# A two-layer transformer kernel: attention heads regrouped over row and column quarters of TensorE, softmax of layer 0 normalised at the output, and a new written order

## What is computed

```python
# layer 0: 16 heads of 16
h = ln(x) * (scale1 + 1) + shift1
q, k, v = split(h @ Wqkv.T + bias)
qn = q / norm(q) * sm ; kn = k / norm(k)
p = softmax(qn @ kn.T + attn_bias) ; x = x + ((p @ v) @ Wproj.T + bproj) * gamma1
u = (ln(x) * (scale2 + 1) + shift2) @ Wfc1.T + bfc1
x = x + (gelu_tanh(u) @ Wfc2.T + bfc2) * gamma2
# layer 1: 8 query heads of 32, one key/value head
h = rms(x) * w * (1 + t @ tw.T)
q, k = rope(h @ Wq.T), rope(h @ Wk.T) ; v = h @ Wv.T
x = x + (softmax(q @ k.T / sqrt(32)) @ v) @ Wo.T
h = rms(x) * w2 * (1 + t @ tw2.T)
x = x + (silu(h @ Wg.T) * (h @ Wu.T)) @ Wd.T
```

## Time and profile before

| | before |
|---|---|
| median of 3 runs | 386.43 us |
| lowest and highest | 386.29, 393.18 us |
| span of the profiled execution | 387.1 us |
| mean granted TensorE clock | 0.907 |
| TensorE busy | 326.0 us, 84% |
| VectorE busy | 256.0 us, 66% |
| ScalarE busy, GpSimd busy | 199.8 us each, 52% |

### The profile page before, as it was taken

One profiled execution on the slowest core, in us unless ns is written; L12 is line 12 of the kernel. 1 busy time (PEld: TensorE's weight loads), 2 busy tenths in 40 slices (PEclk: granted clock), 3 DMA queues, 4 the chain that ended last, 5 costly groups with the idle time before them and its releaser, 6 DMA issues.

```text
span 387.1 us, 6924 instructions
## 1 busy us (share of the span) xinstructions
PE 326.0 (84%) x2240; PEld 262.6 (68%) x2240; DVE 256.0 (66%) x652; ACT 199.8 (52%) x681; POOL 199.8 (52%) x363
## 2 busy tenths in 40 slices
PE   4491575788868986998999999789999999998986
PEld 3261353466655875886776888567788888897975
DVE  3774889887889878657868785755864635434250
ACT  3234268657666688877645885643535525322110
POOL 6536958976687788258858655645522401302000
PEclk9985588576988996998999999969999999999999
DMA  7979130000000000002010000000000000000000
GB/s 219 215 242 322 56 128 10 27 2 1 1 2 1 2 3 1 2 2 54 3 55 0 2 3 1 3 0 0 2 1 3 14 15 0 15 14 2 28 2 27
DMA packets 14035, 14.27 MB, mean 37 GB/s; under 512 B 1568, under 2 KB 12960, under 8 KB 14000
## 3 DMA queue, kind: packets, MB, share of 16 engines
q1 hardware_dynamic: 14000, 13.83, 12.0%
HBM read 12.76 MB, written 1.06 MB: 36 GB/s over the span
## 4 chain that ended last, share of the span: by engine, by line
PE 61%; DVE 16%; POOL 10%; issue 6%; DMA 3%; SPq 2%; ACT 2%; DVEq 0%; POOLq 0%; ACTq 0%
PE ps_linear L1377 16%; PE ps_hidden L1200 7%; PE ps_output L1337 6%; PE ps_hidden L1202 5%; PE ps_hidden L1201 5%; PE ps_scores L1307 5%; PE ps_probs L1314 4%; PE ps_linear L1347 3%; DVE z L1115 2%; DVE qk_pack L1053 2%; DMA res_bias<-in_bfc 2%; PE ps_linear L1200 2%; PE ps_turn L1228 1%; DVE xn L978 1%; PE ps_linear L1202 1%
## 5 line engine op out<-in xcount | busy, mean ns | idle before, releaser
L733 POOL TENSOR_TENSOR z<-z,row_inv 128x512 f32<-128x512 f32 (+1 forms) x64 | 54.8, 859 | 61.8 <-DVE row_inv L1129 61.7
L836 ACT ACTIVATE z<-z,neg_max 128x128 f32<-128x128 f32 x128 | 49.6, 391 | 19.9 <-DVE neg_max L1118 19.8
L848 ACT ACTIVATE probsT<-ps_probs 128x512 f32<-128x512 f32 (+1 forms) x64 | 31.0, 485 | 35.3 <-PE ps_probs L1314 35.1
L1314 PE MATMUL ps_probs<-ident,z 128*128 128x128 f32 x192 | 36.6, 305 | 7.1 <-POOL z L733 6.3
L884 ACT ACTIVATE g_a<-ps_hidden 128x256 f32<-128x256 f32 x32 | 12.3, 384 | 45.7 <-PE ps_hidden L1202 45.5
L697 POOL TENSOR_TENSOR h_lo<-xn,h_hi 128x256 fp32r<-128x256 f32 x32 | 25.9, 812 | 18.0 <-ACT h_hi L799 17.8
L1314 PEld LDWEIGHTS ps_probs<-ident,z 128*128 128x128 f32 x192 | 25.5, 157 | 13.0 <-issue 9.6
L1377 PE MATMUL ps_linear<-Wfc2T,g_h 128*128 128x256 f32 x128 | 31.7, 404 | 1.0 <-DVE res_t L1142 0.8
L1377 PE MATMUL ps_linear<-WdT,g_h 128*128 128x256 f32 x128 | 29.4, 383 | 3.2 <-DVE g_h L1171 2.7
L839 ACT ACTIVATE z<-ps_scores,neg_max_s 128x128 f32<-128x128 f32 x64 | 23.0, 368 | 14.5 <-DVE neg_max_s L1123 14.4
L1377 PEld LDWEIGHTS ps_linear<-Wfc2T,g_h 128*128 128x128 f32 x128 | 25.1, 201 | 5.9 <-DVE res_t L1142 1.0
(11 more groups left out here) (150 smaller groups left out, 973.5 us busy)
## 6 DMA issues: line engine op xcount, KB each, us to landing
gamma<-gamma_scratch SPq DMA_DIRECT2D x8, 256.0 KB, 4.2
stage<-in_Wada SPq DMA_DIRECT2D x6, 256.0 KB, 7.2
X<-in_x SPq DMA_DIRECT2D x4, 256.0 KB, 6.9
stage<-in_Wqkv SPq DMA_DIRECT2D x4, 256.0 KB, 5.0
Wfc2T<-in_Wfc SPq DMA_DIRECT2D x1, 1024.0 KB, 11.0
stage<-in_Wfc SPq DMA_DIRECT2D x4, 256.0 KB, 6.2
WdT<-in_Wd SPq DMA_DIRECT2D x1, 1024.0 KB, 6.5
stage<-in_Wg SPq DMA_DIRECT2D x4, 256.0 KB, 2.7
```

The costliest lines, as they stand in the source:

```text
L733: pool.tensor_tensor(z[:, d, 0:U, :], z[:, d, 0:U, :], row_inv[:, d, 0:U].unsqueeze(2).to_broadcast([P, U, P]), ALU.mult).then_inc(probs_r ...
L836: ins = act.activation(z[:, d, u, :], z[:, d, u, :], ACT.Exp, bias=neg_max[:, d, u:u + 1], accum_out=total)
L848: act.activation(probsT[:, G % 2, 0:U, :], bank_of(key)[:, 0:U * P].rearrange("p (u q) -> p u q", u=U), ACT.Copy).then_inc(is_freed(key)[0 ...
L1314: ins = pe.transpose(bank[:, u * P:(u + 1) * P], z[:, G % DEEP, u, :], ident[:, :])
```

## The change

- Scores: one step U makes two groups. They lie in two row quarters and go to two banks (`ps_scores[0]`, `ps_scores[1]`), and the calls alternate between the two. The two banks are filled and freed together. 32 steps in all, 16 a layer, for 64 before.
- Groups: layer 0 has four groups of four heads an item as before, layer 1 two groups of four heads for four groups of two. The heads of a group are chosen so that the values go to four column quarters in turn.
- Softmax in layer 0: VectorE adds the mask (`mask_add`) and takes the maximum (`row_max`), now two steps; GpSimd adds the negated maximum to z (`max_off`); ScalarE takes one exponential over the whole group without sums. The probabilities are turned unnormalised. `values` multiplies them by v and, in a second part, by a block of ones, so that the row sums come to lie in the output bank beside the output; VectorE inverts them and multiplies (`attn_norm`, in the place of `attn_copy`). `row_inverse` and `norm_probs` are left in layer 1 only.
- Layer 1: the factor 1/sqrt(32) is put into Wq when the chunk is split, and the scaling of the maxima goes.
- `norm_mod` of layer 0 moves from VectorE to ScalarE. `gelu_poly` goes; `gelu_inner` does its work in one fused operation, and the constant goes into the scale of the tanh.
- Waits on the item two before become waits on the last item of the same layer. Rows of Wproj and Wo are permuted on the host, outside the timed program.
- The assumed durations, all due times (`ATT_BASE`, `MLP_BASE`, `CHUNK_SHIFT`, `SHIFT`) and the assumed time for a wake-up are new, and so is the order on every engine. Of `SHIFT`, which is not printed: qk_sum goes from -55.5 to -267.0, qk_root from -6.5 to -47.0, weight_high from 29.5 to 835.0, weight_low from -14.5 to -1.0, and max_off is -44.0.

```diff
-ATT_BASE = [-163.5, -31.5, 33.5, 66.5, 63.0, 93.0, 88.0, 127.0]
-MLP_BASE = [-0.9, 42.5, 89.5, -132.5, 129.5, 140.5, 103.5, 230.0]
-CHUNK_SHIFT = {'Wkv': -113.5, 'tw2': -105.0, 'tw1': 45.0, 'Wfc1': -217.0, 'ada': 48.0, 'Wq': 21.5, 'Wqkv':
-    40.5, 'Wg': -8.5, 'Wu': -138.0}
+ATT_BASE = [-86.0, -62.0, -34.0, 2.5, 2.5, 16.5, 160.5, 383.5]
+MLP_BASE = [-93.5, 19.5, 31.0, 48.5, 150.0, -670.5, 498.0, 828.5]
+CHUNK_SHIFT = {
+    'Wfc1': 2080.5, 'Wkv': 257.0, 'Wq': 77.0, 'Wg': -1910.0, 'Wu': 360.0, 'Wqkv': 255.0, 'ada': -45.5,
+    'tw1': -1095.5, 'tw2': 880.0}
...
-              "scores": ["scores0", "scores1"], "probs": ["probs"], "output": ["output"]}
+              "scores": ["scores"], "probs": ["probs"], "output": ["output"]}
...
-WAKE = 0.19
+WAKE = 0.26
...
-def heads_of(group):
-
-    i = group % 4
-    tiles = H0 // 4 if layer_of(group // 4) == 0 else H1 // 4
-    return [4 * g + i for g in range(tiles)]
+GROUPS = [(n, u, b) for n in range(2 * len(ROUNDS)) for u in range(2) for b in range(2 - layer_of(n))]
+
+
+def groups_of(n):
+    return [G for G, g in enumerate(GROUPS) if g[0] == n]
+
+
+def heads_of(G):
+
+    n, u, b = GROUPS[G]
+    if layer_of(n) == 0:
+        return [4 * g + 2 * u + b for g in range(4)]
+    return [4 * g + 2 * u + c for c in range(2) for g in range(2)]
 
 
...
+            for G in groups_of(n):
+                _, u, b = GROUPS[G]
+                big, U = layer == 0, 2 * n + u
+                first, last = G == groups_of(n)[0], groups_of(n)[-1]
+                g = base + 5 + GROUP_US * (4 * j + 2 * u + b)
+                if b == 0:
+                    add(("scores", U), "PE", 0.62 if big else 0.6, [ready, prev(("scores",), U)], "scores", at=g)
+                if big:
+                    add(("mask_add", G), "DVE", 0.62, [("scores", U), prev(("row_max",), G, 2), prev(("probs_turn",), G, DEEP)]
+                        + ([("mask_add", G - 1)] if b else []), frees=("scores", U) if b else None, at=g)
+                    add(("row_max", G), "DVE", 0.62, [("mask_add", G), prev(("row_max",), G)], at=g)
+                    add(("max_off", G), "Pool", 1.0, [("row_max", G)], at=g)
+                else:
+                    add(("row_max", G), "DVE", 0.68, [("scores", U), prev(("row_max",), G), prev(("probs_turn",), G, DEEP)],
+                        at=g)
+                add(("exp", G), "ACT", 0.55 if big else 1.45, [("max_off" if big else "row_max", G), prev(("exp",), G)],
+                    frees=None if big else ("scores", U), at=g)
+                if not big:
+                    add(("row_inverse", G), "DVE", 0.085, [("exp", G), prev(("row_inverse",), G)], at=g)
+                    add(("norm_probs", G), "Pool", 1.0, [("row_inverse", G), prev(("norm_probs",), G)], at=g)
+                add(("probs_turn", G), "PE", 0.535, [("exp" if big else "norm_probs", G), prev(("probs_turn",), G)],
                     "probs", at=g)
...
-                add(("values", G), "PE", 0.35 if big else 0.18, [("probs_copy", G), prev(("values",), G)]
-                    + ([("v_copy", n)] if big else []), "output" if i == 0 else None, at=g)
+                add(("values", G), "PE", 0.62 if big else 0.35, [("probs_copy", G), prev(("values",), G)]
+                    + ([("v_copy", n)] if big else []), "output" if first else None, at=g)
...
+            add(("attn_copy", n), "DVE" if layer == 0 else "ACT", 0.75 if layer == 0 else 0.27, [("values", last), prev(("attn_copy",), n), prev(("project",), n, 2)],
...
+            for e in range(2):
+                for half in range(2):
+                    pool.memset(ones_pad[:, e, half * D0:(half + 1) * D0], 1.0 if half == e else 0.0)
...
+            def max_off(G):
+                d = G % DEEP
+                pool.wait_ge(max_ready, G + 1)
+                pool.tensor_tensor(z[:, d, :, :], z[:, d, :, :], neg_max[:, d, :].unsqueeze(2).to_broadcast([P, 4, P]),
+                                   ALU.add).then_inc(max_taken, 1)
+
             def norm_probs(G):
-                U, d = len(heads_of(G)), G % DEEP
-                pool.wait_ge(inv_ready, G + 1)
-                pool.tensor_tensor(z[:, d, 0:U, :], z[:, d, 0:U, :],
-                                   row_inv[:, d, 0:U].unsqueeze(2).to_broadcast([P, U, P]),
+                d = G % DEEP
+                pool.wait_ge(inv_ready, group_ord(G) + 1)
+                pool.tensor_tensor(z[:, d, :, :], z[:, d, :, :], row_inv[:, d, :].unsqueeze(2).to_broadcast([P, 4, P]),
                                    ALU.mult).then_inc(probs_ready, 1)
 
...
+                if CHUNKS[c][0] == "Wq":
+                    act.activation(raw, raw, ACT.Copy, scale=SCORE_SCALE1).then_inc(wq_scaled, 1)
+                    act.wait_ge(wq_scaled, 1)
...
+                    dst, src = h_full[:, m, j, ft, :], bank_of(key)[:, ft * P:(ft + 1) * P]
+                    if layer_of(n) == 0:
+                        ins = act.activation(dst, src, ACT.Identity, bias=modul[:, first + 1, ft, s:s + 1],
+                                             scale=modul[:, first, ft, s:s + 1])
...
-                key = ("scores", G)
+                d = G % DEEP
+                if layer_of(GROUPS[G][0]) == 0:
+                    act.wait_ge(max_taken, group_ord(G) + 1)
+                    act.activation(z[:, d, :, :], z[:, d, :, :], ACT.Exp).then_inc(exp_ready, 1)
+                    return
                 act.wait_ge(max_ready, G + 1)
-                d = G % DEEP
-                for u in range(len(heads)):
-                    total = row_sum[:, d, u:u + 1]
-                    if layer_of(n) == 0:
-                        ins = act.activation(z[:, d, u, :], z[:, d, u, :], ACT.Exp,
-                                             bias=neg_max[:, d, u:u + 1], accum_out=total)
-                    else:
-                        ins = act.activation(z[:, d, u, :], bank_of(key)[:, u * P:(u + 1) * P], ACT.Exp,
-                                             bias=neg_max_s[:, d, u:u + 1], scale=SCORE_SCALE1, accum_out=total)
+                for u in range(4):
+                    ins = act.activation(z[:, d, u, :], ps_scores[u // 2][:, (u % 2) * P:(u % 2 + 1) * P], ACT.Exp,
+                                         bias=neg_max[:, d, u:u + 1], accum_out=row_sum[:, d, u:u + 1])
                 ins.then_inc(exp_done(G)[0], 1)
...
-                    act.activation(g_a[:, o % 2, :], g_a[:, o % 2, :], ACT.Tanh, scale=GELU_C).then_inc(g_tanh, 1)
+                    act.activation(g_a[:, o % 2, :], g_a[:, o % 2, :], ACT.Tanh, scale=GELU_CUBE).then_inc(g_tanh, 1)
...
+            def mask_add(G):
+                b, key = GROUPS[G][2], scores_key(G)
                 if G >= DEEP:
...
+                if b == 0:
+                    dve.wait_ge(*is_filled(key))
+                ins = dve.tensor_tensor(z[:, G % DEEP, :, :], ps_scores[b][:, :].rearrange("p (u k) -> p u k", u=4),
+                                        bias_mask[:, :].unsqueeze(1).to_broadcast([P, 4, P]), ALU.add)
+                ins.then_inc(mask_added, 1)
+                if b == 1:
+                    dve.wait_ge(mask_added, group_ord(G) + 1)
+                    dve.sem_inc(is_freed(key)[0], 1)
+
+            def row_max(G):
+                d = G % DEEP
+                if layer_of(GROUPS[G][0]) == 0:
+                    dve.wait_ge(mask_added, group_ord(G) + 1)
+                    dve.tensor_reduce(neg_max[:, d, :], z[:, d, :, :], AX_X, ALU.max, negate=True).then_inc(max_ready, 1)
+                    return
+                if G >= DEEP:
+                    dve.wait_ge(*is_filled(("probs_turn", G - DEEP)))
+                dve.wait_ge(*is_filled(scores_key(G)))
+                for b in range(2):
+                    ins = dve.tensor_reduce(neg_max[:, d, 2 * b:2 * b + 2],
+                                            ps_scores[b][:, 0:2 * P].rearrange("p (u k) -> p u k", u=2), AX_X, ALU.max,
+                                            negate=True)
+                ins.then_inc(max_ready, 1)
...
+            def attn_norm(n):
+                key, o = ("values", groups_of(n)[0]), ord0(n)
+                dve.wait_ge(*values_done(n))
+                dve.reciprocal(o_inv[:, :], bank_of(key)[:, C:2 * C]).then_inc(sum_inverted, 1)
+                dve.wait_ge(sum_inverted, o + 1)
+                if n >= 2:
+                    dve.wait_ge(*is_filled(("project", n - 2)))
+                dve.tensor_tensor(o_full[:, n % 2, :, :].rearrange("p c q -> p (c q)"), bank_of(key)[:, 0:C],
+                                  o_inv[:, :], ALU.mult).then_inc(is_freed(key)[0], 1)
...
-                dve.wait_ge(g_poly, o + 1)
-                dve.tensor_tensor(g_a[:, o % 2, :], g_b[:, o % 2, :], g_u[:, o % 2, :], ALU.mult
-                                  ).then_inc(g_inner, 1)
+                dve.wait_ge(g_squared, o + 1)
+                dve.scalar_tensor_tensor(out=g_a[:, o % 2, :], in0=g_a[:, o % 2, :], scalar=1.0 / 0.044715,
```

(56 more changed lines are left out.)

256 lines of the change are left out of this document (112 added, 144 removed), and 3 rows, old and new, of the table SHIFT.

## The result

The changed kernel took 361.84 us (median of 4 runs, 360.58 to 363.13) beside 386.36 us for the kernel before (384.68 to 393.18). The ratio is 0.937, 95% interval 0.931 to 0.942: faster by 6.3%. The forecast was 346; the result lies in its range, at the number of rival C (362). The profiled execution has a span of 361.3 us, 25.8 less than before's.

A forecast was written before the change was run, and what follows sets the result against it. The prediction took a ring of waits among the vector engines to bound layer 0 and TensorE to bound layer 1. It summed 387.1 - 24.9 (layer 1) - 12 (layer 0) - 4 (start) = 346.2, so 346 us, range 328 to 368.

The forecast's parts named there:

- rival C: Layer 0 doesn't shrink: savings become waits on GpSimd's queue, TensorE stays longer at 1.2 GHz; 362 us, chance 0.20.
- TensorE in layer 1, 24.9 us: Layer 1's regrouped steps shorten TensorE: scores by 10.1 us, values by 12.6, turns by 2.2.
- the halving: Layer 1 values: four column quarters at once halve the time again, as two did, to 0.33 us a step.
- A microsecond less of TensorE is a microsecond less of span: Layer 1 stretch, 195 to 350 us: TensorE busy 150 of 155 us, so its savings count fully.
- The vector engines in layer 0, 12 us: Layer 0, 45 to 195 us: 12 us less, from two reckonings of 13 and 11 us.
- the ring: Layer 0's chain of waits among vector engines: 1.2 us less a group from maximum to turn, 13 us if it bounds.
- a floor: Layer 0's output normalisation: inverse and product of 128x256 priced at 0.418 us each, 6.7 us in all, as a minimum.
- The start, 4 us: Before the first turn of q: new ranks recover 4 of TensorE's 9.5 us idle.
- TensorE in layer 0, 0: Layer 0's TensorE wins on scores and losses on values cancel: 0, with ends 7 us less and 12 more.
- Rival B: Score banks filled and freed as one pair make TensorE wait: up to 70 us more, 416 us; chance 0.05.
- The new order: All new ranks across the kernel: beyond the start, not costed from the trace, only widening the range.
- A: Quarters don't overlap further: layer 1 gives 12.7 us, layer 0's values cost 7; 365 us, chance 0.10.

The follow-up runs named there:

- e4_old_ranks: The changed kernel's work with the due times and wake-up time of the kernel before; 384.87 us, ratio 0.997 to the kernel before.
- e13_l1_scores_twice: The changed kernel with every layer 1 score matmul issued twice, same result; 365.11 us, ratio 0.943 to the kernel before.
- e1_copy_sums: The changed kernel with a plain copy in place of attn_norm's inverse of the row sums, written order kept; 357.99 us, ratio 0.927 to the kernel before.
- e11_replanned: The changed kernel's work in another order, searched by replay with its measured durations, WAKE 0.20; 357.68 us, ratio 0.924 to the kernel before.
- e14_l0_scores_twice: The changed kernel with every layer 0 score matmul issued twice; 365.29 us, ratio 0.945 to the kernel before.

## Why the prediction held, and where it failed

- **TensorE in layer 1, 24.9 us: right in size.** From one step each, scores take 10.2 us for 20.2 (0.64 a step), values 5.6 for 17.9 (0.35), turns 8.0 for 11.8 (0.50 a step, 0.60 assumed), 26.1 us in all. Summed over all steps of the two traces it is less: scores 11.5 for 20.4, since two steps fell at the lower clock, values 6.2 for 18.0, and the turns of both layers together 28.9 for 30.8; that is 22.6 us. With the four fc1 blocks that left this stretch (6 us) it accounts for the 29.8 us by which the busy time there fell. Four column quarters do overlap as the two did: 0.35 us is nearer to the halving's 0.33 than to the 0.39 that the prediction estimated from the factors of the Trainium skill, TensorE: Matmul & The Clock Gate, Part 3, though 0.04 us a step is 0.6 us in all and decides nothing. The same part says that weight loads overlap running matmuls only where the row group differs; that doesn't hold for these four column quarters, whose eight loads and eight matmuls on the same rows fit in 0.35 us.
- **"A microsecond less of TensorE is a microsecond less of span": wrong as a rule.** The stretch behind layer 0 did shrink by 26.8 us. But the same work in the old order gave 1.5 us in all (e4_old_ranks), and a known dose of 7.6 us moved the end by 3.3 (e13_l1_scores_twice; it was given to the new kernel, where the stretch is 91% full, and adds work, where the change took it out). A stretch that is 97% full is full because the order lays work there; taking work out leaves idle time unless the order is made anew for it.
- **The vector engines in layer 0, 12 us: the step that failed.** Layer 0 ended 1.2 us later than before. It took 6 us of MLP work more; counted one for one, it in effect gained some 5 of the 12 and of the start's 4 together, and 11 us are missing. Both ways of reckoning the 12 failed. The first took the ring: it got shorter by 1.2 us in the shortest group and 2.8 on average, no less than was forecast, but 32 x 1.2 / 3 = 13 us holds only "if the ring is the bound", and it was not: VectorE waited 1.7 us in all for a free buffer of z before the change. The second took VectorE's work, forecast 8.9 us less. By its rows it is 1.8 us more (in: 14.0 and 3.4 for the normalisations, 1.3 for the fused GELU step; out: 11.5 and 5.4), since the inverse, priced at 0.42 as "a floor", takes 1.748, 10.6 us more over eight. And where e1_copy_sums takes these 10.7 us out again, layer 0 ends only 3.7 us earlier and the time falls by 3.8: dividing VectorE's work by its 81% to get time overrates it threefold. That the two ways agreed was no evidence: both assumed that one limit sets layer 0, and a microsecond of VectorE or of TensorE is worth some 0.4 there. What the rest of the 11 us is, beyond the 3.8 of the inverse and what a better order recovers (4 us, e11_replanned), isn't settled. The trace shows where to look: in the new kernel no maximum of layer 0 starts between 150.5 and 167.6 us, and the chain that ended last runs in that stretch through the inverse norms of a later sequence on GpSimd (to 154.0), their packing on VectorE and their turns. The longest such gap before was 11.7 us; but e11_replanned, which is faster, has one of 20.7, so the gaps alone don't set the time.
- **Rival C** has the right number and half the right reason. Layer 0 didn't shrink, and ScalarE waits for GpSimd's max_off in its place (27.8 us). The clock was the same at 45 to 120 us (0.75) and lower at 120 to 195 (0.88 for 0.93). But C called layer 1's gain of 25 us safe, and in the old order the stretch behind layer 0 got 17.1 us shorter, 6 of them by work moved ahead, while layer 0 grew by 13 (e4_old_ranks).
- **The start, 4 us:** 2.6 measured at the first turn of q. **TensorE in layer 0, 0:** its steps came as the better ends had it (0.55 for sixteen scores, 0.57 for the values with sums); 32 x 0.54 to 16 x 0.55 is 8.5 us less, more than the "up to 7.4" of the prediction, whose own lower step of 0.54 gives 8.7. But a dose there is worth some 0.4 per microsecond (e14_l0_scores_twice), not 0.
- **Rival B** is real and small: 4.9 us of TensorE idle in front of scores in the new order, 12.0 in the old, 2.5 in the kernel before with its separate banks, none in e11_replanned (1.1 on its weight loads).
- **The new order** was what I left out as not to be costed. It is worth 23 us on the new work (384.87 to 361.84) and minus 9 on the old (386.4 to 395.5). The prediction summed the work's gains as if the order came along; it did. That the time fell in the range is in part luck: the range reached up to 368 for the sake of C and A, and the one term that was left out is as large as the whole gain.

Of the 15 us between the profiled span and its forecast, 11 are missing ahead of layer 0's end, 3 are more idle time of TensorE behind it, and 1 is the rest.

## What to carry to other kernels

Where an order is fixed at build time, a change of the work and the order made for it are one change: try the work in the old order and the old work in the new order before giving the gain to either, and search an order for the old work too. Price a new operation only from a row with its kind and its element count; a row of the same shape and another operation can be off by four. A stretch that is nearly full shows where work lies, not what a microsecond there is worth; a known dose of work measures that.

## What the runs showed of the hardware

- VectorE's RECIPROCAL of 128x256 fp32 from PSUM took 1.748 us, a COPY of the same 0.415, a RECIPROCAL of 128x4 0.177: some 6.2 ns an element of the row between the two inverses, where the copy has 1.6 in all. The Trainium skill, VectorE: DVE Perf Modes, First, the fixed hardware budget, says that Reciprocal runs as an iterated hardware divide with a repeat count of 8. The trace agrees in so far as the inverse costs some four times the copy for each element; it shows no count.
- Four column quarters in fp32: eight instructions in 0.35 us, where four in one quarter took 0.56.
- Two row quarters in fp32 overlap also when one quarter's calls are all issued ahead of the other's (0.65 and 0.64 us for the step); in fp16 the alternation matters (0.79 and 0.55, the same in all steps at full clock to within 0.07).
- The same score steps at the two levels of the granted clock: sixteen fp16 instructions 0.55 us at 2.4 GHz and 0.96 to 1.03 at 1.2 GHz, eight fp32 instructions 0.64 and 1.15 to 1.22.
